# A two-layer expert block with attention: weight and table loads in another order, and slot scatters grouped elsewhere

## The chip, the cores and the metric

The kernel runs on one core of a Trainium2 chip. The metric is the device time of one execution in microseconds. TensorE (PE) multiplies matrices, PEld is its weight load, VectorE is DVE, ScalarE is ACT, GpSimd is POOL and SyncE is SP. SP issues plain transfers from its queue; POOL issues the indirect ones (gathers, scatters, scatter-adds).

## The reference

```python
x = L0_attn_x                                  # 8 x 1024 tokens x 256, float32
x = x + 0.5 * ffn(layernorm(x), router_w, w1, w2, bias)
x = x + attn(layernorm(x), w_qkv, w_gated, w_proj, gn_weight, gn_bias)
x = x + 0.5 * ffn(layernorm(x), router_w, w1, w2, bias)

def ffn(x, router_w, w1, w2, bias):            # 8 experts, top 2, capacity tokens / 8 = 1024 each
    scores = softmax(xf @ router_w)
    expert_weights, top_experts = top_k(scores, 2)
    for k in range(2):
        # the first 1024 tokens of each expert, in token order
        h = gelu(einsum('ech,ehf->ecf', xe, w1))      # 256 -> 1024
        ye = einsum('ecf,efh->ech', h, w2)            # 1024 -> 256
        out += scatter_add(ye) * expert_weights[:, k][:, None]
    return out + bias
```

The attention is a retention layer: 16 heads of 16, rotated queries and keys, a decaying causal mask without a softmax, a group norm over each head and all of time, a gate silu(x @ w_gated.T) and a projection.

## The kernel before

The kernel has three stages one after another on one core: the first expert layer, the attention, the second expert layer. The normalisation and routing of the first layer come before it; those of the second are part of the attention stage.

**The expert stages.** `ffn(r)` exists once for each engine, with r = 0 and r = 1. The work is 16 passes over an expert (8 experts for the first choice, then 8 for the second), 2 groups of 512 slots each: 32 groups. A loop `pair(p)` covers GE = 4 groups j, that is two experts, and runs 8 times. The products are made in split form (a high and a low part in fp32r).

- *SP* loads w1 and w2 of the coming expert pass into `stg1` and `stg2` (1 MB each, one buffer each), and the slot table of a coming group into `tab[:, j]` (32 KB). `next_w1(q, e)` waits until the eight slices of w1 of pass q-1 have been split (`f.w1l`), `next_w2(q, e)` the same for w2. The table of group j is loaded again for the next loop once `f.add` says that this group's scatter-add has landed. All of it is in one queue, in program order.
- *POOL*, in `pair`: `gather` reads the 512 rows of the group three ahead into `xe` (4 indirect transfers, line 428), when the table has landed and TensorE has read the old rows; `add` adds the group's results to the output rows (4 transfers, line 447), when they have been weighed and the adds before have landed. In the first three loops (`late`) `second_slot` weaves in the scatters of the second choice's slot entries (line 381), six per group until all 64 are out.
- *PE*, in `pair`: for each of 8 slices fj the down-products of group g (line 650, 12 matmuls) and the up-products of group g+1 (line 639, 6 matmuls); after slice 5 the transposes of the gathered rows of group g+2 (line 628). `up` of slice fj waits for the GELU of slice fj-2, whose PSUM bank it takes.
- *ACT*, in `pair`: per slice the GELU of group g+1 (line 1105), then in even groups the cast of a slice of w1 of the next pass (line 1109), in odd groups of w2 (line 1112). Before the first of each eight it waits for the raw weights, `f.w1raw` or `f.w2raw`. At the end of a group it weighs and evacuates the results (line 1122).
- *DVE* makes the low parts: of the weights (lines 1664, 1668), of the rows (1659) and of the hidden values (1672, 1676).

With r = 1 the last two batches' output rows are also stored by SP at the start of the stage (`output_store`, line 339); the last one waits for POOL's `half_bias(B - 1, j)`, which stands behind the second gather.

**The attention stage.** Each engine has a hand-written order `sequence(b)`, run for b = -1 to 7, and then `drain()`. A sequence works on batch b's eight tiles n and, between them, on the front of batch b+1, the output of batch b-1 and the routing of b-2. On POOL the order holds:

- `rotated(n)` (line 490), the last addition of the rotation of queries and keys; it waits for VectorE's products, and TensorE's `turn(n)` waits for it;
- the small powers of the norms (line 374), `half_bias` (line 393);
- `slots(b, j)` (line 381): two of the eight slot scatters of a batch's first choice. `slots(b, 0)` first waits for `R[1].pay`, which VectorE gives with the slot numbers `idx` (line 1598, in `slot_entries`). The scatters are wanted only by the second expert stage.

VectorE issues `slot_entries(1, b - 2)` right behind `rotate(n + 7)`.

Of the kernel before, what the change touches and what calls it, by code (L numbers as in the profile page):

```python
# [11 lines left out]
B, T, C = 8, 1024, 256  # L12
N = B * T
NT = T // P
# [4 lines left out]
E, TOPK, FF = 8, 2, 1024  # L19
# [5 lines left out]
NP = TOPK * E // 2  # L25
# [52 lines left out]
def macaron_kernel(nc, x_in, w_qkv, w_gated, w_proj, gn_w, gn_b, router_w, w1, w2, f_bias,  # L78
# [3 lines left out]
    with ctx:  # L82
# [113 lines left out]
        def held(eng, sem, value):  # L196

            eng.wait_ge(sem, value)
            eng.sem_inc(S0.passed, 1)
# [5 lines left out]
        def _(sp):  # L205
# [64 lines left out]
            def ffn(r):  # L270
                f = F[r]
                tab_t = slot_d[r].rearrange("(g p t) w -> g p t w", p=P, t=GT)

                def next_w1(q, e):
                    sp.wait_ge(f.w1l, q * FJ)
                    sp.dma_start(stg1[:], w1_t[e, :, :, :]).then_inc(f.w1raw, 16)

                def next_w2(q, e):
                    sp.wait_ge(f.w2l, q * FJ)
                    sp.dma_start(stg2[:], w2_t[e, :, :, :]).then_inc(f.w2raw, 16)  # L280

                def pair(p, wraps):

                    for j in range(GE):
                        q = p * 2 + j // 2 + 2
                        if j % 2 == 0:
                            next_w1(q, q - wraps)
                        else:
                            next_w2(q, q - wraps)

                        held(sp, f.add, p * (GE * GT * 16) + (j + 1) * GT * 16)
                        sp.dma_start(tab[:, j, :, :], tab_t[p * GE + GE + j, :, :, :]).then_inc(tabs[j], 16)

                tabs = [f.tab0, f.tab1, f.tab2, f.tab3]
                if r == 0:
                    sp.wait_ge(S0.acc_z, 16)
                    sp.wait_ge(S0.out_z, 16)
                    sp.wait_ge(S0.xn_z, 16)
                sp.wait_ge(R[r].scat, B * NT * 16)
                for j in range(GE):  # L300
                    sp.dma_start(tab[:, j, :, :], tab_t[j, :, :, :]).then_inc(tabs[j], 16)
                next_w1(1, 1)
                next_w2(1, 1)
                if r == 1:
                    output_store(B - 2)
                    output_store(B - 1)
                with sp.Fori(0, NP // 2 - 1) as p:
                    pair(p, 0)
                sp.wait_ge(R[r].scat1, B * NT * 16)
                pair(NP // 2 - 1, E)  # L310
                with sp.Fori(NP // 2, NP - 1) as p:
                    pair(p, E)

            ffn(0)

# [19 lines left out]
            def output_store(b):  # L336

                sp.wait_ge(R[1].half, (b + 1) * (NT // 2))
                sp.dma_start(out_w[b, :, :, :], rows_of(b)[:]).then_inc(R[1].stored, 16)
# [17 lines left out]
            ffn_weights(1)  # L357
            residual_store(B - 1)
            ffn(1)
            sp.wait_ge(F[1].add, NG * GT * 16)  # L360

# [4 lines left out]
        def _(pool):  # L366
# [9 lines left out]
            def scatter(r, b, some):  # L376

                if 0 in some:
                    held(pool, R[r].pay, b + 1)
                for n in some:  # L380
                    pool.indirect_dma_start(  # L381
                        out=slot_d[r], out_offset=bass.IndirectOffsetOnAxis(ap=idx[:, b, n:n + 1], axis=0),
                        in_=pay_rows[:, b, 2 * n:2 * n + ROW], in_offset=None, bounds_check=SLOTS - 1, oob_is_err=False)\
                        .then_inc(R[r].scat if n < NT else R[r].scat1, 16)

            def half_bias(b, j):

                if not 0 <= b < B:
                    return
                pool.wait_ge(R[1].xn, b * NT + 2 * j + 2)  # L390
                two = slice(2 * j, 2 * j + 2)
                x = rows_of(b)
                pool.tensor_tensor(x[:, two, :], x[:, two, :], hbias[:].unsqueeze(1).to_broadcast([P, 2, C]), ALU.add).then_inc(R[1].half, 1)
# [89 lines left out]
            def rotated(n):  # L483

                if not 0 <= n < B * NT:
                    return
                pool.wait_ge(A.qk_r, n + 1)
                if n >= 2:
                    pool.wait_ge(A.st, 2 * (n - 2) + 2)
                pool.tensor_tensor(qk[:, n % 2, :], rt1[:, n % 2, :], rt2[:, n % 2, :], ALU.add).then_inc(A.roped, 1)  # L490

            def first_output(b):

                if not 0 <= b < B:
                    return
                pool.wait_ge(A.y_r, b * NT + 1)
                if b >= 1:
                    pool.wait_ge(A.yg, b * KC)
                pool.tensor_copy(yT[:, :, 0:P], y0[:]).then_inc(A.moved, 1)

            def head_power(b):

                if not 0 <= b < B:
                    return
                pool.wait_ge(A.v_r, nth[1]["variances", b, 0])
                pool.tensor_tensor(gsm[:, 3, :], gsm[:, 2, :], K_["mhalf"][:, 0:KC], ALU.pow).then_inc(A.grs, 1)

            def front_power(b):
                if 0 <= b < B:
                    power(A, lnf, b)  # L510

            def residual_power(b):
                if 0 <= b < B:
                    power(R[1], lnr, b)

            def slots(b, j):

                if 0 <= b < B:
                    scatter(1, b, (2 * j, 2 * j + 1))

            def sequence(b):

                n = b * NT
                rotated(n + 2)
                head_power(b - 1)
                half_bias(b - 2, 2)
                rotated(n + 3)
                first_output(b)
                half_bias(b - 2, 3)
                rotated(n + 4)  # L530
                slots(b - 3, 1)
                rotated(n + 5)
                front_power(b + 1)
                slots(b - 3, 2)
                rotated(n + 6)
                slots(b - 3, 3)
                rotated(n + 7)
                rotated(n + 8)
                residual_power(b - 1)
                slots(b - 2, 0)  # L540
                rotated(n + 9)
                half_bias(b - 1, 0)
                half_bias(b - 1, 1)

            def drain():

                head_power(B - 1)
                for j in range(1, NT // 2):
                    slots(B - 3, j)
                residual_power(B - 1)  # L550
                for j in range(NT // 2):
                    slots(B - 2, j)
                for j in range(NT // 2):
                    slots(B - 1, j)
                half_bias(B - 2, 2)
                half_bias(B - 2, 3)

            pool.wait_ge(S0.slot1, 16)
            for b in range(-1, B):
                sequence(b)  # L560
            drain()
            ffn(1)

# [1565 lines left out]
```

## Time and profile before

| | |
|---|---|
| three runs | 2357.43, 2367.85 and 2370.43 us (median 2367.85) |
| the profiled execution | 2357.43 us, of which the span of the trace is 2355.6 |
| granted TensorE clock, mean | 0.975 |
| PE, PEld busy | 91%, 80% |
| DVE, ACT, POOL busy | 57%, 43%, 50% |
| first expert stage, attention, second expert stage | about 150 to 930, 930 to 1560, 1560 to 2356 us |

All times in the rows are microseconds from the span's start, unless marked ns. In a row of the timeline the number behind the start is how long the work took; "x8" joins eight instructions, and the bracket says how long the engine stood idle before it and who ended that. `L428` is line 428 of the kernel. In a row of stretches the numbers are the busy time of PE, PEld, DVE, ACT and POOL with the number of instructions, then the granted clock, the busy share of the 16 transfer engines and GB/s.

### The profile page before, as it was taken

To read this page: it belongs to the slowest core of one execution; us is meant where nothing else is said; L and a number is where in the kernel's file an instruction comes from. 1 tells how busy PE (TensorE), PEld (TensorE's weight loads), DVE (VectorE), ACT (ScalarE), POOL (GpSimd) and SP (SyncE) were. 2 spreads that over 40 slices of the span, in tenths; PEclk is the share of its full clock that TensorE was granted. 3 is DMA by queue.
4 is the path that set the end of the run, shared out by engine and by line. 5 is a ranking of instruction groups with operands and counts; after the bars stand their busy time and mean duration, and the time that the engine had idled before them with its cause. 6 is when DMAs were issued, how large, how long until landed. Compare 5 with 4: busy or idle time off the path is not lost.

```text
span 2355.6 us, 57424 instructions
## 1 busy us (share of the span) xinstructions
PE 2154.4 (91%) x22468; PEld 1894.0 (80%) x22468; DVE 1341.5 (57%) x3312; ACT 1008.1 (43%) x2149; POOL 1169.9 (50%) x911
## 2 busy tenths in 40 slices
PE   6749999999999996899999999729999999999997
PEld 5739998899999996677777777529998899999997
DVE  7745555455555552578778887635554455555552
ACT  4433443444444441446555555324343344444442
POOL 4754667654444443223344454364766764444443
PEclk9999999999999998999999999859999999999999
DMA  8532343444344433112111121132434354434342
GB/s 336 192 104 68 80 100 82 81 109 100 81 101 82 99 62 79 58 39 74 57 57 58 57 76 75 57 120 50 94 81 97 81 111 86 97 84 98 83 82 28
DMA packets 129223, 209.41 MB, mean 89 GB/s; under 512 B 24876, under 2 KB 105328, under 8 KB 122864
## 3 DMA queue, kind: packets, MB, share of 16 engines
q0 software_dynamic: 57344, 69.21, 17.6%
q1 hardware_dynamic: 71696, 137.62, 16.7%
q8 instruction: 132, 2.16, 0.4%
q14 instruction: 51, 0.42, 0.1%
HBM read 136.03 MB, written 72.88 MB: 89 GB/s over the span
## 4 chain that ended last, share of the span: by engine, by line
PE 40%; issue 6%; POOL 5%; DVE 4%; DMA 3%; ACT 1%; POOLq 0%; another core or an unknown queue 0%; SPq 0%; DVEq 0%; ACTq 0%
PE bank L639 10%; PE bank L650 10%; PE bank L723 10%; PE bank L811 3%; POOL out_rows L447 2%; POOL slot_table L381 2%; DMA out_rows<-yb,tab 2%; PE bank L844 2%; PE bank L779 1%; PE bank L794 1%; PE bank L829 1%; PE bank L628 1%; PE bank L883 1%; DMA tab<-slot_table 1%; POOL xe L428 1%
## 5 line engine op out<-in xcount | busy, mean ns | idle before, releaser
L1105 ACT ACTIVATE h<-bank 128x512 f32<-128x512 f32 x512 | 305.9, 597 | 873.5 <-PE bank L639 804.2
L1672 DVE CAST hh<-h 128x512 fp32r<-128x512 f32 x512 | 224.1, 438 | 715.3 <-ACT h L1105 628.1
L650 PE MATMUL bank<-w2h,hh 128*128 128x256 f32 x2048 | 582.5, 284 | 0.0
L650 PE MATMUL bank<-w2h,hl 128*128 128x256 f32 x2048 | 579.8, 283 | 0.0
L650 PE MATMUL bank<-w2l,hh 128*128 128x256 f32 x2048 | 579.7, 283 | 0.0
L428 POOL DMA_INDIRECT xe<-xn_rows,tab x256 | 274.8, 1073 | 344.5 <-issue 225.4
L639 PE MATMUL bank<-xh,w1h 128*128 128x512 f32 x1024 | 406.6, 397 | 4.2 <-DVE xl L1659 4.2
L650 PEld LDWEIGHTS bank<-w2h,hh 128*128 128x128 f32 x2048 | 391.5, 191 | 19.1
L639 PE MATMUL bank<-xl,w1h 128*128 128x512 f32 x1024 | 405.7, 396 | 0.0
L650 PEld LDWEIGHTS bank<-w2l,hh 128*128 128x128 f32 x2048 | 391.7, 191 | 17.1
L639 PE MATMUL bank<-xh,w1l 128*128 128x512 f32 x1024 | 399.8, 390 | 0.0
L650 PEld LDWEIGHTS bank<-w2h,hl 128*128 128x128 f32 x2048 | 391.5, 191 | 0.0
L1676 DVE TENSOR_TENSOR hl<-h,hh 128x512 fp32r<-128x512 f32 x512 | 350.4, 684 | 1.1
L381 POOL DMA_INDIRECT slot_table<-pay,idx x256 | 289.2, 1130 | 100.7 <-issue 75.1
L447 POOL DMA_INDIRECT out_rows<-yb,tab x128 | 211.3, 1651 | 171.2 <-issue 146.7
L447 POOL DMA_INDIRECT acc<-yb,tab x128 | 211.3, 1651 | 169.2 <-issue 109.3
L490 POOL TENSOR_TENSOR qk<-rt 128x512 f32<-128x512 f32 x64 | 88.4, 1381 | 287.0 <-DVE rt L1753 252.8
L639 PEld LDWEIGHTS bank<-xh,w1l 128*128 128x128 f32 x1024 | 193.2, 189 | 44.3
L639 PEld LDWEIGHTS bank<-xh,w1h 128*128 128x128 f32 x1024 | 195.2, 191 | 30.1 <-issue 4.9
L639 PEld LDWEIGHTS bank<-xl,w1h 128*128 128x128 f32 x1024 | 195.2, 191 | 21.5
L628 PE MATMUL bank<-cst,xe 128*128 128x128 f32 x512 | 69.2, 280 | 64.0 <-DMA xe<-xn_rows,tab 64.0
L628 PEld LDWEIGHTS bank<-cst,xe 128*128 128x128 f32 x512 | 60.9, 144 | 74.9 <-issue 54.8
(209 smaller groups left out, 3311.2 us busy)
## 6 DMA issues: line engine op xcount, KB each, us to landing
stg<-in_L_ffn_w SPq DMA_DIRECT2D x64, 1024.0 KB
xb<-acc SPq DMA_DIRECT2D x9, 1024.0 KB, 8.3
xa<-in_L_attn_x SPq DMA_DIRECT2D x8, 1024.0 KB, 14.1
xn_rows<-xa SPq DMA_DIRECT2D x8, 1024.0 KB
xn_rows<-xn_r SPq DMA_DIRECT2D x8, 1024.0 KB
xr<-acc SPq DMA_DIRECT2D x7, 1024.0 KB
out_rows<-xr SPq DMA_DIRECT2D x7, 1024.0 KB
slot_table<-pay,idx POOLq DMA_INDIRECT x256
```

Of the source, the lines that this page charges most:

```text
L381: pool.indirect_dma_start(out=slot_d[r], out_offset=bass.IndirectOffsetOnAxis(ap=idx[:, b, n:n + 1], axis=0), in_=pay_rows[:, b, 2 * n:2 * ...
L428: pool.indirect_dma_start(out=xe[j % 2][:, t, :], out_offset=None, in_=xn_d, in_offset=bass.IndirectOffsetOnAxis(ap=tabu[:, j, t, 0:1], ax ...
L447: pool.indirect_dma_start(out=dst, out_offset=bass.IndirectOffsetOnAxis(ap=tabu[:, j, t, 0:1], axis=0), in_=yb[j % 2][:, t, :], in_offset= ...
L490: pool.tensor_tensor(qk[:, n % 2, :], rt1[:, n % 2, :], rt2[:, n % 2, :], ALU.add).then_inc(A.roped, 1)
L628: last = pe.transpose(bank[6 + k][:, t * P:(t + 1) * P], xe[j % 2][:, t, k * P:(k + 1) * P], ident)
L639: last = pe.matmul(bank[fj % 2][:], a[:, k, w], c[j % 2][:, k, :], start=(n == 0), stop=(n == 5))
L650: last = pe.matmul(o, a[:, fj, s], c[:, fj, :], start=(fj == 0 and n == 0 and t % 2 == 0), stop=(fj == FJ - 1 and n == 2), skip_group_chec ...
L723: last = pe.matmul(out, a(k), c(k), start=(n == 0), stop=(n == 3 * KC - 1))
L811: last = pe.matmul(bank[3 + x][s, half * P:(half + 1) * P], qkT[rows, n % 2, KC + half, s], qm[rows, n % 2, half, :, s], start=True, stop= ...
L1105: act.activation(h32[fj % 2][:], bank[fj % 2][:], ACT.Gelu_apprx_tanh).then_inc(f.gelu, 1)
L1672: dve.tensor_copy(hh[:, fj, :], h32[fj % 2][:]).then_inc(f.hh, 1)
L1676: dve.tensor_tensor(hl[:, fj, :], h32[fj % 2][:], hh[:, fj, :].bitcast(fp32), ALU.subtract).then_inc(f.hl, 1)
```

## The change

It has two independent parts, both a new order of the same instructions.

*SP, in the expert stages.* Before, the weight loads run ahead of the loop by w1(1) and w2(1), and in the loop w1(2p+2), table 0, w2(2p+2), table 1, w1(2p+3), table 2, w2(2p+3), table 3 follow. After, only w1(1) is ahead of the loop, and the loop has w2(2p+1), table 0, w1(2p+2), table 1, w2(2p+2), table 2, w1(2p+3), table 3; w2(15) stands behind the last loop. With r = 1 the two output stores therefore come ahead of w2(1).

*POOL, in the attention stage.* In each sequence three pairs of scatters of batch b-3, which stood singly behind rotated(n+4), (n+5) and (n+6), are gone. Three pairs of batch b-2 stand together behind rotated(n+7), and the fourth where the first was. The drain has one batch's three pairs less.

```diff
                     for j in range(GE):
-                        q = p * 2 + j // 2 + 2
+                        q = p * 2 + j // 2
                         if j % 2 == 0:
-                            next_w1(q, q - wraps)
+                            next_w2(q + 1, q + 1 - wraps[j])
                         else:
-                            next_w2(q, q - wraps)
+                            next_w1(q + 2, q + 2 - wraps[j])
...
                 next_w1(1, 1)
-                next_w2(1, 1)
                 if r == 1:
                     output_store(B - 2)
                     output_store(B - 1)
                 with sp.Fori(0, NP // 2 - 1) as p:
-                    pair(p, 0)
+                    pair(p, (0, 0, 0, 0))
                 sp.wait_ge(R[r].scat1, B * NT * 16)
-                pair(NP // 2 - 1, E)
+                pair(NP // 2 - 1, (0, E, E, E))
                 with sp.Fori(NP // 2, NP - 1) as p:
-                    pair(p, E)
+                    pair(p, (E, E, E, E))
+                next_w2(TOPK * E - 1, E - 1)
...
                 rotated(n + 4)
-                slots(b - 3, 1)
                 rotated(n + 5)
                 front_power(b + 1)
-                slots(b - 3, 2)
                 rotated(n + 6)
-                slots(b - 3, 3)
                 rotated(n + 7)
+                slots(b - 2, 0)
+                slots(b - 2, 1)
+                slots(b - 2, 2)
                 rotated(n + 8)
                 residual_power(b - 1)
-                slots(b - 2, 0)
+                slots(b - 2, 3)
                 rotated(n + 9)
...
                 head_power(B - 1)
-                for j in range(1, NT // 2):
-                    slots(B - 3, j)
                 residual_power(B - 1)
```

## Rows read from the trace of the kernel before

**Rows 1.** Busy time in one stretch of the first expert stage.

```profile
200.00:300.00 100.00, 100.00 (x649) 90.97 (x648) 52.57 (x112) 42.21 (x96) 64.80 (x51) 1.00 0.40 87
```

**Rows 2.** Timeline of ACT: weighings that end groups, in both stages.

```profile
202.52 1.56 ACT L1122 ACTIVATE yb<-bank,tab 128x256 f32<-128x256 f32 x4
...
466.50 1.56 ACT L1122 ACTIVATE yb<-bank,tab 128x256 f32<-128x256 f32 x4
...
1621.91 1.56 ACT L1122 ACTIVATE yb<-bank,tab 128x256 f32<-128x256 f32 x4
...
1785.99 1.56 ACT L1122 ACTIVATE yb<-bank,tab 128x256 f32<-128x256 f32 x4
...
1886.53 1.56 ACT L1122 ACTIVATE yb<-bank,tab 128x256 f32<-128x256 f32 x4
```

**Rows 3.** Timeline of SP: issues of tables, weights and an output store.

```profile
471.71 0.34 SPq L292 DMA_DIRECT2D tab<-slot_table  x1
...
1567.85 0.58 SPq L339 DMA_DIRECT2D out_rows<-xr  x1
...
1638.85 0.36 SPq L292 DMA_DIRECT2D tab<-slot_table  x1
...
1715.89 0.33 SPq L292 DMA_DIRECT2D tab<-slot_table  x1
...
1867.39 0.33 SPq L292 DMA_DIRECT2D tab<-slot_table  x1
1868.04 0.38 SPq L276 DMA_DIRECT2D stg<-in_L_ffn_w  x1
1891.70 0.33 SPq L292 DMA_DIRECT2D tab<-slot_table  x1
...
1969.41 0.33 SPq L292 DMA_DIRECT2D tab<-slot_table  x1
```

**Rows 4.** Timeline of PE: first transposes of the two expert stages.

```profile
160.78 1.94 PE L628 MATMUL bank<-cst,xe 128*128 128x128 f32 x8 [21.61 <-DMA xe<-xn_rows,tab]
...
1579.63 1.94 PE L628 MATMUL bank<-cst,xe 128*128 128x128 f32 x8 [32.55 <-DMA xe<-xn_rows,tab]
```

**Rows 5.** Short stretches behind the weights issued at 1868.04.

```profile
1871.00:1872.00 1.00, 1.00 (x9) 0.93 (x8) 0.00 (x0) 0.55 (x2) 0.69 (x2) 1.00 1.00 414
...
1873.00:1873.50 0.50, 0.50 (x4) 0.41 (x3) 0.45 (x1) 0.00 (x0) 0.29 (x1) 1.00 0.00 0
```

**Rows 6.** Timeline of ACT: the start of group 2, second stage.

```profile
1647.37 0.60 ACT L1105 ACTIVATE h<-bank 128x512 f32<-128x512 f32 x1 [0.46 <-PE bank L639]
1647.87 0.41 ACT L1109 ACTIVATE w1h<-stg 128x256 fp32r<-128x256 f32 x1
1650.19 0.60 ACT L1105 ACTIVATE h<-bank 128x512 f32<-128x512 f32 x1 [1.92 <-PE bank L639]
```

**Rows 7.** Timeline of POOL: the first group's fourth gather, both stages.

```profile
155.96 1.01 POOL L428 DMA_INDIRECT xe<-xn_rows,tab  x1 [0.30 <-issue]
...
1571.76 1.01 POOL L428 DMA_INDIRECT xe<-xn_rows,tab  x1 [0.30 <-issue]
```

**Rows 8.** The chain that ended last: a fourth gather in group 10.

```profile
1875.98 2.82 DMA xe<-xn_rows,tab
```

**Rows 9.** Timeline of DVE and POOL in two batches of the attention stage.

```profile
1191.55 0.98 POOL L381 DMA_INDIRECT slot_table<-pay,idx  x1 [0.30 <-issue]
...
1197.87 0.17 DVE L1598 TENSOR_TENSOR idx<-sel 128x16 uint32<-128x16 f32 x1
...
1198.09 1.26 POOL L490 TENSOR_TENSOR qk<-rt 128x512 f32<-128x512 f32 x1 [1.22 <-PE bank L794]
1215.05 1.31 POOL L490 TENSOR_TENSOR qk<-rt 128x512 f32<-128x512 f32 x1 [15.70 <-DVE rt L1753]
...
1249.88 2.77 DVE L1856 TENSOR_TENSOR ygl<-yg,ygh 128x1024 fp32r<-128x1024 f32 x1
...
1253.17 2.06 DVE L1856 TENSOR_TENSOR ygl<-yg,ygh 128x1024 fp32r<-128x1024 f32 x1
```

## The prediction

> **What bounds the kernel now.** I read the page first, then the time in stretches of 100 us, then the dates of three engines inside the two expert stages, and last what TensorE waits for.
>
> The stretches say where to look. In the expert stages TensorE is busy for 100 of every 100 us [rows 1], except at their ends and in one stretch of each, which the next view sizes. So a moved transfer costs nothing there until somebody stands still for it, and the places to read are the few where TensorE does.
>
> ScalarE ends each group of 512 slots with the weighing at line 1122. In the second expert stage the first weighing starts at 1621.91 and the eighth at 1785.99: 164.08 / 7 = 23.44 us a group, TensorE's own pace. The twelfth should start at 1621.91 + 11 x 23.44 = 1879.75 and starts at 1886.53: 6.8 us are lost up to there. In the first stage the same sum is 202.52 + 11 x 23.44 = 460.36 against 466.50: 6.1 us lost [rows 2]. These 12.9 us are all that this stretch of the two stages has to give.
>
> They come from GpSimd's cycle. While the second choice's slot scatters are woven in (groups 0 to 10), a group takes GpSimd longer than 23.44 us. Sync issues the reload of a table the moment the scatter-add before it has landed, so the dates of the reloads are the cycle: from 1638.85 (group 0) to 1891.70 (group 10) it is 252.85 / 10 = 25.29 us [rows 3]. In this stretch GpSimd falls back 1.85 us per group against TensorE, and at the end the gathered rows come too late.
>
> The tables are not late because of the weights: at 1867.39 Sync issues the table, and at 1868.04 the weights behind it, which had been free to go [rows 3]. What holds the tables there is the adds.
>
> The other stop is at the start of a stage. TensorE stands still for 32.55 us before the first transposes of the second stage, and a gather ends that wait [rows 4].
>
> **The change, Sync's part.** Per loop it issues the same 4 weight loads and 4 table loads. Today the load that stands ahead of the table of group g is the one that ScalarE wants at the start of group g+3 (at the loop's entry g+2), so it has a group to spare. After the change the load wanted at the start of group g+2 is issued behind the table of group g. Nothing is queued behind a waiting weight load that suffers, since its own condition (the old weights split) is long true. The new thing is that weights wait for a scatter-add.
>
> When would they land? The weights issued at 1868.04 behind the table of 1867.39 show as 414 GB/s at 1871, and at 1873.0 the transfer engines are empty [rows 5]. From the table's issue to landed weights: 5.6 us.
>
> When are they wanted? The first cast of w1 for group 2 is at 1647.87 [rows 6], so for group 12 it is at 1647.87 + 10 x 23.44 = 1882.27 without a stall. That cast follows the weighing's date by 1647.87 - (1621.91 + 23.44) = 2.52; for the first stage it is due at 202.52 + 2.52 + 11 x 23.44 = 462.88.
>
> What covers a late arrival? ScalarE has made the group's first GELU before it waits. TensorE can still do the second and third up-products and the down-products up to the fourth: two steps of 1650.19 - 1647.37 = 2.82 us [rows 6], and about half a step, 1.4 us, for the last down-product, together 7.0. Of these 0.5 has passed when the cast normally starts; the cast (0.41) and a GELU (0.60) must still fit in. That leaves 5.5, and I allow 0.2 of it for hand-overs: 5.3 us.
>
> I expect a gain in the cycle itself. In the first three intervals weights run beside GpSimd's transfers, (1715.89 - 1638.85) / 3 = 25.68 us; in the seven after them they follow the table as they will after the change, (1891.70 - 1715.89) / 7 = 25.12 [rows 3]. I take 3 x 0.56 = 1.7 us off by group 10, once per stage. Bounds: nothing, and 3.
>
> Second stage, group 12: 1891.70 - 1.7 + 5.6 - 5.3 - 1882.27 = 8.0 us of lateness, in place of 6.8: +1.2. First stage: 471.71 - 1.7 + 5.6 - 5.3 - 462.88 = 7.4 in place of 6.1: +1.3. The two waits don't add: TensorE stops a little in each of groups 7 to 12 for the weights, and then the gathered rows are in time. Bounds per stage: no added lateness, and the cover absent (+5.3). I take the middle because the cover is read from a steady rhythm. Once the scatters are done, the weights are early: the table of 1969.41 (group 14) puts them at 1975.0, and group 16 wants them at 1882.27 + 6.78 + 4 x 23.44 = 1982.8.
>
> **The start of the second stage.** Sync now issues both output stores there before w2(1). Today w1, w2 and an output store (1 MB each) are issued within 1 us, the last at 1567.85 [rows 3]. The fourth gather of the first group, issued at 1571.76, lets TensorE begin at 1579.63: 7.87 us. In the first stage only w1 and w2 lie beside it, and the same step takes 160.78 - 155.96 = 4.82 us [rows 4, 7]. After the change w2(1) waits behind the last store, which waits for GpSimd's bias additions until some 11 us after the gather, so 2 MB lie beside the gathers here too. I take 7.87 - 4.82 = 3.0 us off, all on the path, since the chain runs through this landing. Bounds: nothing (if the store is the slow part), and 7.87 less the 2.82 of such a gather with little beside it [rows 8], 5.0. w2(1) is wanted over 40 us later, so its own delay costs nothing.
>
> The Trainium skill (DMA: Bandwidth & Descriptors, "Issuing engines are not separate DMA queues") says that transfers issued from different engines interleave on the same 16 transfer engines. This trace agrees: the same gather takes 4.82 us beside 2 MB of Sync's and 7.87 beside 3. With a path of its own for the gathers this term would be zero.
>
> **The change, GpSimd's part.** In each batch of the attention stage six slot scatters move: they were three pairs in the next batch, and now stand together behind the rope addition n+7. They need the batch's slot numbers, written at 1197.87, while that addition starts at 1198.09. The next rope addition starts at 1215.05 and waits for VectorE until then [rows 9]. A scatter is 0.98 us with 0.30 ahead of it [rows 9], so six are about 7.7 us, from 1199.4 to 1207.1, in a gap of 15.7. Cost: 0, hidden behind VectorE's and TensorE's own work. With that cover gone TensorE would wait up to 7.7 us in each of 6 batches. The pair left behind keeps its place, and at the stage's end GpSimd has six scatters less in a stretch where it then waits for VectorE's variance: 0.
>
> Where the scatters leave, they lay beside VectorE's subtraction at line 1856, which takes 2.77 us, while its twin takes 2.06 [rows 9]. I count nothing, because TensorE runs through that stretch.
>
> The Trainium skill (SBUF — State Buffer, "Who interferes with whom") says that a VectorE instruction with two SBUF inputs and a GpSimd instruction that reads SBUF exclude each other. The stretched row agrees in kind. What the rule would give is the third rival.
>
> **Sum.** +1.3 + 1.2 - 3.0 = -0.5 us on the profiled execution (span 2355.6, time 2357.43): 2356.9. That execution is the lowest of three runs; their median is 10.4 above it. Applied to the median: 2367.85 - 0.5 = 2367.3. I call up to 0.5% (11.8 us) no change, about what a measurement here can tell: the three runs lie 13 us apart.
>
> **The rivals.**
> 1. *The late weights stay hidden*, and the gathers still end last. Only the start's gain is left: -3.0, 2364.8. For it: the added lateness is just over 1 us a stage. Against it: it needs 1.3 us more cover. Chance 0.17.
> 2. *Slower: the late weights find no cover.* If TensorE stops as soon as ScalarE waits, each stage loses 5.3 us more: -0.5 + 10.6 = +10.1, 2378.0; with the cycle's gain absent too, 3.4 more, 2381.4. It decides from the first group whose weights land behind the due cast, group 5 or 6. For it: ScalarE's wait holds up every later GELU. Against it: the order of TensorE's instructions. Chance 0.19, three quarters of it beyond 0.5%.
> 3. *The scatters' collision was on the path.* 2.77 - 2.06 = 0.7 us in each of 5 batches, -3.5: 2363.8. Against it: TensorE's busy share there. Chance 0.10.
> 4. *Faster: GpSimd's cycle falls to TensorE's pace* once weights no longer run beside its adds. Then the 12.9 us of both stages vanish, and the start's 3.0: 2352. It needs 1.85 us off every group. Against it: in the last seven intervals the weights already lie there, and the cycle is 25.12. Chance 0.10.
>
> My forecast has 0.44. With rivals 1 and 3 and a quarter of rival 2 this makes 0.76 for within 0.5%; 0.14 slower, 0.10 faster.
>
> **Range.** Downwards: rival 1 with the start at its bound and rival 3 on top, -8.5, gives 2359.4; I go to the lowest run shown, 2357. Upwards rival 2, to 2381. Rival 4 and the end of rival 2 are left out, under 2 in 10. The likeliest case alone spans 2363 to 2371.
>
> **What would show it.** Right: in groups 7 to 12 ScalarE's first cast waits for a transfer of weights, and TensorE stops just before the fourth up-product; its waits for gathered rows before group 12 are gone; the twelfth weighing is 7 to 9 us late; the fourth gather is followed by TensorE after about 5 us; the rope additions n+7 and n+8 stay some 17 us apart. Wrong: a twelfth weighing over 12 us late (no cover) or under 5 (the cycle changed), or a later rope addition n+8.

## The result, and the profile after

| | before | after |
|---|---|---|
| median | 2369.14 us (4 runs) | 2401.78 us (4 runs) |
| ratio | | 1.0145, interval 1.0122 to 1.0167 |
| the profiled execution, its span | 2357.43, 2355.6 | 2399.01, 2397.2 |

The changed kernel is slower by 32.6 us in the medians, where I had forecast -0.5. It is outside the range. By dates in the two traces the 41.6 us between the two spans lie as follows. Up to the first load of the attention stage (932.78 before, 937.01 after): +4.2. From there to the last slot numbers of VectorE (1549.75, 1589.13): +35.2. From there to the first weighing of the second expert stage: -1.4. The rest of that stage: +3.6.

The expert stages first. These rows answer to [rows 2, 3]: weighings of ScalarE, tables and weights of Sync, of the changed kernel.

```profile
203.17 1.56 ACT L1120 ACTIVATE yb<-bank,tab 128x256 f32<-128x256 f32 x4
...
470.12 1.56 ACT L1120 ACTIVATE yb<-bank,tab 128x256 f32<-128x256 f32 x4
...
1659.90 1.56 ACT L1120 ACTIVATE yb<-bank,tab 128x256 f32<-128x256 f32 x4
...
1927.92 1.56 ACT L1120 ACTIVATE yb<-bank,tab 128x256 f32<-128x256 f32 x4
```

```profile
219.54 0.36 SPq L292 DMA_DIRECT2D tab<-slot_table  x1
...
348.47 0.34 SPq L292 DMA_DIRECT2D tab<-slot_table  x1
348.90 0.38 SPq L280 DMA_DIRECT2D stg<-in_L_ffn_w  x1
...
472.60 0.34 SPq L292 DMA_DIRECT2D tab<-slot_table  x1
```

The twelfth weighing is 470.12 - 203.17 - 11 x 23.44 = 9.1 us late in the first stage and 10.2 in the second, where [rows 2] had 6.1 and 6.8. The cycle of the tables is (472.60 - 219.54) / 10 = 25.31 in the first stage and 25.35 in the second, no shorter than before (25.27 and the 25.29 of [rows 3]).

What the view of waits says of ScalarE in the changed kernel (engine, tile, line, who ended the wait: us in total, times, longest):

```profile
ACT w2h L1110 <- DMA stg<-in_L_ffn_w: 53.9, 10, 8.4
...
ACT w1h L1107 <- DMA stg<-in_L_ffn_w: 42.8, 10, 6.7
...
ACT vz L1195 <- remote: 38.7, 6, 7.1
```

The first two rows are the forecast's late weights. The third is new, and it comes six times, once for each batch whose scatters moved. "remote" is the profile's word for a releaser that it can't name. GpSimd in one of these batches, the answer to [rows 9]:

```profile
1211.33 1.29 POOL L490 TENSOR_TENSOR qk<-rt 128x512 f32<-128x512 f32 x1 [3.59 <-PE bank L792]
1213.54 1.05 POOL L381 DMA_INDIRECT slot_table<-pay,idx  x1 [0.92 <-DVE idx L1596]
...
1220.01 0.97 POOL L381 DMA_INDIRECT slot_table<-pay,idx  x1 [0.30 <-issue]
```

Six scatters stand from 1213.54 to 1220.98, as forecast in number, length and place. The next rope addition starts at 1234.79, 23.5 us behind the one of 1211.33, where [rows 9] had 1215.05 - 1198.09 = 17.0. The distances in the five batches that have both are 24.5, 23.5, 23.4, 22.1 and 23.9. GpSimd is not the late one: the scatters end 13.8 us before that addition, and GpSimd then waits for VectorE. The other three engines, in the same batch:

```profile
1215.54 0.48 ACT L1207 ACTIVATE qm<-bank,cst 128x256 f32<-128x256 f32 x1
...
1216.29 0.21 DVE L1771 TENSOR_TENSOR state<-bank,cst 128x64 f32<-128x64 f32 x1
1216.32 0.45 PE L809 MATMUL bank<-qm,qkT 32*64 32x128 f32 x3 [0.31 <-issue]
...
1217.08 0.41 PE L809 MATMUL bank<-qm,qkT 32*64 32x128 f32 x2 [0.30 <-issue]
...
1218.25 0.28 PE L721 MATMUL bank<-wTh,xnl 128*128 128x256 f32 x1
...
1219.22 0.39 PE L721 MATMUL bank<-xnh,wTl 128*128 128x512 f32 x1 [0.45 <-issue]
...
1222.23 0.69 DVE L1761 TENSOR_TENSOR aw<-bank,cst 128x512 f32<-128x512 f32 x1 [5.73 <-remote]
1222.31 0.38 ACT L1195 ACTIVATE vz<-bank 128x256 f32<-128x256 f32 x1 [6.29 <-remote]
...
1222.84 0.36 PE L721 MATMUL bank<-wTh,ygh 128*128 128x256 f32 x1 [2.29 <-ACT vz L1195]
```

VectorE's product at line 1761 and ScalarE's copy at line 1195 wait for counts of TensorE alone. TensorE has made what they want by 1217.5 and 1218.5, but both start within 0.1 us of each other at 1222.2, some 4 us late and 1.2 us after the last scatter has ended. TensorE meanwhile goes in pieces, with gaps that nothing explains. The chain that ended last runs through it:

```profile
1215.65 0.36 ACT qm L1207
1216.02 6.27 another core or an unknown queue
...
1222.31 0.39 ACT vz L1195
```

The hold isn't the whole of the 6.5 us by which this distance grew. TensorE had stood idle or gone in pieces from 1216 on, and then its granted clock fell (the number behind the brackets of POOL):

```profile
1223.00:1224.00 1.00, 1.00 (x9) 1.00 (x9) 0.97 (x4) 1.00 (x3) 0.00 (x0) 0.99 0.00 0
1224.00:1225.00 1.00, 1.00 (x23) 0.78 (x29) 0.12 (x1) 0.16 (x1) 0.00 (x0) 0.50 0.00 0
...
1227.00:1228.00 1.00, 1.00 (x21) 0.86 (x21) 0.33 (x1) 0.62 (x2) 0.00 (x0) 0.81 0.00 0
```

That is 3.4 us at half clock with TensorE fully busy, which costs 1.7 us. The clock fell to half in all five batches (for 3.4 us in three of them, for some 10 us in the first and the last); before, it stayed at 1.00 between the two additions of [rows 9].

The start of the second expert stage answers to [rows 4, 7]:

```profile
1611.19 1.01 POOL L428 DMA_INDIRECT xe<-xn_rows,tab  x1 [0.30 <-issue]
```

```profile
1616.71 1.51 PE L626 MATMUL bank<-cst,xe 128*128 128x128 f32 x6 [30.24 <-DMA xe<-xn_rows,tab]
```

From the fourth gather to TensorE it is 5.5 us now, 7.9 before.

### The profile page after: what moved, and what is told of

Read it like the earlier page. It is cut to its first block, busy times and chain, and to the rows that moved or that the text cites. A ratio compares the mean times of both kernels' runs of the same rounds, so it can differ in the third digit from the quotient of the medians.

```text
span 2397.2 us, 57448 instructions
## 1 busy us (share of the span) xinstructions
PE 2179.2 (91%) x22468; PEld 1910.7 (80%) x22468; DVE 1343.5 (56%) x3312; ACT 1008.4 (42%) x2149; POOL 1151.6 (48%) x911
## 4 chain that ended last, share of the span: by engine, by line
PE 39%; issue 6%; POOL 5%; DVE 4%; DMA 3%; another core or an unknown queue 2%; ACT 1%; POOLq 0%; SPq 0%; DVEq 0%; ACTq 0%
PE bank L637 10%; PE bank L648 10%; PE bank L721 9%; PE bank L809 3%; POOL out_rows L447 2%; POOL slot_table L381 2%; DMA out_rows<-yb,tab 2%; PE bank L842 2%; PE bank L777 1%; PE bank L792 1%; PE bank L881 1%; PE bank L626 1%; PE bank L827 1%; DMA tab<-slot_table 1%
## 5 line engine op out<-in xcount | busy, mean ns | idle before, releaser
L381 POOL DMA_INDIRECT slot_table<-pay,idx x256 | 271.0, 1059 | 105.0 <-issue 75.4
L1666 DVE TENSOR_TENSOR w2l<-stg,w2h 128x256 fp32r<-128x256 f32 x256 | 106.0, 418 | 53.7 <-issue 30.7
L1662 DVE TENSOR_TENSOR w1l<-stg,w1h 128x256 fp32r<-128x256 f32 x256 | 106.0, 419 | 42.7 <-ACT w1h L1107 31.5
```

The lines of the kernel that those rows point to most:

```text
L381: pool.indirect_dma_start(out=slot_d[r], out_offset=bass.IndirectOffsetOnAxis(ap=idx[:, b, n:n + 1], axis=0), in_=pay_rows[:, b, 2 * n:2 * ...
L1662: dve.tensor_tensor(w1l[:, :, w], stg1[:, :, w], w1h[:, :, w].bitcast(fp32), ALU.subtract).then_inc(f.w1l, 1)
L1666: dve.tensor_tensor(w2l[:, fj, :], stg2[:, fj, :], w2h[:, fj, :].bitcast(fp32), ALU.subtract).then_inc(f.w2l, 1)
```

## The experiments

Kernels that ran together, on one chip and beside the kernel before, are called a set here. It matters, because the sets turned out to be of two kinds. The differences within a set count, not those between sets.

### The two parts alone, the scatters spread, and a busy GpSimd (set 1)

e1 has only Sync's part of the diff, e2 only GpSimd's.

> Only the new order of Sync's loads; the attention stage as before. The profile of the changed kernel puts the loss of the expert stages at +3.5 and +3.5 us, 0.7 ahead of them, and the start of the second stage at -2.4: +5 us on the kernel before if the two parts of the change are independent. If instead the late weights only hurt together with the shifted attention stage, 0 or below.

> Only the new places of GpSimd's slot scatters; Sync's order as before. If the six scatters behind rotated(n+7) cost 5.9 us in each of six batches: +35 us, and the waits of ScalarE at vz and VectorE at aw that end on no named engine are there six times each. If the attention stage lost its time to Sync's part: 0.

e3 has the scatters early but pair by pair:

```diff
                 half_bias(b - 2, 2)
+                slots(b - 3, 2)
                 rotated(n + 3)
                 first_output(b)
                 half_bias(b - 2, 3)
+                slots(b - 3, 3)
                 rotated(n + 4)
-                slots(b - 3, 1)
                 rotated(n + 5)
                 front_power(b + 1)
-                slots(b - 3, 2)
                 rotated(n + 6)
-                slots(b - 3, 3)
                 rotated(n + 7)
+                slots(b - 2, 0)
                 rotated(n + 8)
                 residual_power(b - 1)
-                slots(b - 2, 0)
+                slots(b - 2, 1)
```

The pairs of the last batches in the drain follow suit.

> The scatters of batch b-2 start as early as in the changed kernel, behind rotated(n+7), but one pair stands behind each of n+7, n+8, and the two additions that open the next sequence. Theory A, what costs is that six scatters follow each other without a gap: within 4 us of the kernel before. Theory B, what costs is the place, scatters between rotated(n+7) and rotated(n+8): a third of the loss, about +12 us.

e4 leaves the scatters and adds work to GpSimd:

```diff
                 rotated(n + 7)
+                busy(b - 2, 7)
                 rotated(n + 8)
```

`busy(b, 7)` waits for the batch's slot numbers and then issues seven memsets of 128 x 1024.

> The scatters stand where they stood in the kernel before. Behind rotated(n+7) seven memsets of 128x1024 (0.95 us each, about 7 us of GpSimd work that moves nothing by transfer) are added. Theory A (the scatters themselves hold up the other engines): 0 to +3 us. Theory C (GpSimd is busy and something waits for it): about the same +30 to +35 us as six scatters.

| | median us | ratio to the kernel before (2358.25) |
|---|---|---|
| e1 Sync's part | 2361.46 | 1.0012 (1.0000 to 1.0023) |
| e2 GpSimd's part | 2359.98 | 1.0007 (0.9995 to 1.0019) |
| e3 spread | 2369.42 | 1.0055 (1.0036 to 1.0074) |
| e4 memsets | 2358.12 | 1.0003 (0.9990 to 1.0016) |

My first theory (each part keeps its own loss) fell: e2 has the same six scatters and costs nothing. In its trace the rope addition n+7 is at 1205.86 and n+8 at 1222.83, 17.0 us. The kernel before was faster here too, 2358 in place of 2369. With nothing lost in e2, e4 could not tell anything yet. e3's loss is another matter, and an ordinary one: one pair stands directly ahead of the rope addition n+3, ahead of which e2's GpSimd is idle for 1.1 us only. In the traces, about 1175 us, n+3 follows n+2 after 7.0 us in e3 and after 5.6 in e2.

### The changed kernel again, with a shift, and the output stores alone (set 2)

> The changed kernel once more, beside the kernel before on the same chip. Neither part alone cost more than 2.8 us. Theory D, the two parts together cost what neither does: +33 us again, with the same six stops of 6 us behind the six scatters. Theory E, the first comparison was special to its chip or its loading: the sum of the parts, +4 to +8 us.

e6 is the changed kernel with eight fulfilled waits more on Sync ahead of the attention stage.

> The changed kernel with eight more instructions on Sync just ahead of the attention stage (waits that are already fulfilled), which only shift Sync's later code and its place in time by under 1 us. Theory D1, the loss comes from how instruction or semaphore traffic happens to fall against the scatters: a loss clearly other than 33 us, perhaps none. Theory D2, it comes from the order of transfers alone: +33 us again.

```diff
                 next_w1(1, 1)
-                next_w2(1, 1)
                 if r == 1:
                     output_store(B - 2)
                     output_store(B - 1)
+                next_w2(1, 1)
```

> The kernel before, with only the two output stores at the start of the second expert stage moved ahead of w2(1). Loops and scatters as before. The fourth gather should be followed by TensorE after 5.5 us in place of 7.9: -2.4 us. If the gain belonged to the later w2 of the loop, 0.

e8 is e7 with GpSimd's part of the change.

> The same with the scatters where the changed kernel has them. By the sum of the parts +1.7 - 2.4 = about -1 us. If the six scatters stop the engines in any program whose Sync code differs from the one that was measured with them alone: +30 us.

| | median us | ratio to the kernel before (2369.18) |
|---|---|---|
| e5 the changed kernel | 2404.00 | 1.0150 (1.0127 to 1.0173) |
| e6 with the shift | 2405.88 | 1.0159 (1.0142 to 1.0176) |
| e7 stores first | 2368.41 | 0.9996 (0.9985 to 1.0008) |
| e8 the same, six scatters | 2396.49 | 1.0120 (1.0103 to 1.0137) |

The loss is back, and the shift does nothing to it. e8 against e7 is 28 us for the scatters, e5 against e8 is 7.5 us for the loops' order. e7's start takes 1585.29 to 1590.82, 5.5 us, but its median can't be told from the kernel before: 2.2 us are less than such a comparison resolves. e8 and e2 differ in one moved line of Sync's, and e8 loses 27.3 us where e2 lost 1.7. Either that line matters, or the set does.

### GpSimd's part again, with fewer scatters in a row (sets 3 and 4)

> GpSimd's part alone for the second time. In the first call it lost 1.7 us, on a chip where no engine's wait ended on an unnamed releaser; in the second call the same six scatters, with the two output stores moved as well, lost 27 us. Theory F, the chip decides (or where the program lies on it), not the program: where the kernel before takes about 2369 us, +28 to +30 us here too, with six stops; where it takes about 2358, +2. Theory D, this part needs another part of the change to hurt: within 5 us on any chip.

> The scatters of the batch start as early as in the changed kernel, but one pair behind each of four rope additions. Where f1 shows six stops: theory A, a run of six without a gap is what costs: no stop, and the 7 to 11 us that the first call showed for this order, in place of the 28 of f1. Theory B, the scatters in this place cost, each for itself: a third of f1's stops stay behind n+7.

> Scatters as before, and seven memsets of GpSimd behind n+7. Where f1 shows six stops: theory A, only scatters hold up the others: 0 to +3 us. Theory C, a busy GpSimd holds them up: near f1.

f4 has `slots(b - 3, 3)` behind n+6, `slots(b - 2, 0)` and `slots(b - 2, 1)` behind n+7 and `slots(b - 2, 2)` behind n+8.

> Two pairs behind n+7 in place of three; the third pair behind n+6 of the next sequence, the fourth behind n+8. Where f1 shows six stops of 6 us: if the stop grows with the run of scatters past a start, 2 to 4 us per batch, +12 to +24 us. If it is proportional to their number, 4 us per batch, +19 to +24. If it takes more than four in a row, 0 to +3.

> The changed kernel again. If this set is of the kind in which the kernel before takes about 2369 us: +33 us with six stops. If it is of the kind with about 2357: no stops, and only Sync's part is left, +3 to +6 us. A loss of 30 us in a set of the second kind would speak for an effect of the two parts together.

> Two pairs of scatters behind n+7. Where the kernel before takes about 2369 us: +12 to +24 us if the stops grow with the number of scatters, 0 to +3 if it takes more than four in a row. Else 0.

> Seven memsets behind n+7, scatters as before. Where the kernel before takes about 2369 us: 0 to +3 us if only scatters hold up the other engines, about +28 if a busy GpSimd does. Else 0.

| | median us | ratio to the kernel before |
|---|---|---|
| set 3 (before 2356.35): f1 GpSimd's part | 2356.79 | 0.9999 (0.9987 to 1.0011) |
| f2 spread | 2366.11 | 1.0036 (1.0023 to 1.0049) |
| f3 memsets | 2354.74 | 0.9990 (0.9976 to 1.0004) |
| f4 four scatters | 2356.28 | 1.0005 (0.9989 to 1.0021) |
| set 4 (before 2357.13): g1 the changed kernel | 2358.71 | 1.0006 (0.9993 to 1.0019) |
| g2 four scatters | 2358.01 | 1.0001 (0.9989 to 1.0013) |
| g3 memsets | 2359.01 | 1.0003 (0.9990 to 1.0017) |

g1 settles what e2 and e8 left open: the very kernel that lost 33 and 35 us loses 1.6 us here, which can't be told from nothing. It is not the program but the set. Set 3 ran on the same chip as set 2, so it isn't the chip either. ScalarE in g1, in the batch whose addition n+7 is at 1208.12:

```profile
1213.57 0.38 ACT L1195 ACTIVATE vz<-bank 128x256 f32<-128x256 f32 x1 [0.76 <-PE bank L721]
```

The same copy is released by TensorE after 0.76 us, with the same scatters beside it (1210.33 to 1217.77). I call a set *held* when traces in it have waits that end on "remote", and *free* when none has. Held: the first comparison and set 2. Free: sets 1, 3 and 4. But sets 3 and 4 couldn't answer what in a held set does the holding, since nothing was held in them.

### One kernel with another arrangement in each batch (sets 5 and 6)

Here one execution in a held set compares all arrangements. Behind rotated(n+7):

```diff
                 rotated(n + 7)
+                behind7(b - 2)
                 rotated(n + 8)
...
+            def behind7(b):
...
+                if b == 2:
+                    held(pool, R[1].pay, b + 1)
+                    fill(7)
+                elif b == 3:
+                    for j in range(3):
+                        for n in (2 * j, 2 * j + 1):
+                            scatter(1, b, (n,))
+                            fill(1)
+                    del todo[b][:3]
+                elif 0 <= b < B - 2:
+                    for _ in range({0: 3, 1: 2, 4: 1, 5: 3}[b]):
+                        left(b)
```

`fill(k)` issues k memsets of 128 x 1024, each awaited, and `left(b)` the next pair of the batch's scatters. The scatters left over are issued in pairs behind n+8 and n+4 to n+6.

> Behind rotated(n+7) stand, batch after batch: six scatters; four; seven memsets and no scatter; six scatters with a memset of 0.95 us after each; two scatters. The distance from n+7 to n+8 tells what each costs (17.0 us is the undisturbed one, 22.1 to 24.5 the one behind six scatters in the changed kernel's trace). In a set of the kind in which the kernel before takes about 2369 us: theory A, a run without gaps holds up the others once it is longer than some length: 23.5, 17 to 20, 17, 17 and 17 us. Theory A2, each scatter costs 1 us: 23.5, 21, 17, 23, 19. Theory C, a busy GpSimd holds them up: 23.5, 21, 23, 28, 19. In a set of the other kind: 17 in all five.

> The same kernel and the same numbers as for the first run of it: in a set in which the kernel before takes about 2369 us, the distances from n+7 to n+8 behind six scatters, four, seven memsets, six scatters with memsets between and two scatters are 23.5, 17 to 20, 17, 17, 17 us by theory A (a long run without gaps), 23.5, 21, 17, 23, 19 by theory A2 (each scatter costs), 23.5, 21, 23, 28, 19 by theory C (a busy GpSimd). Otherwise 17 in all five.

Set 5 was free (before 2358.18, h1 2354.55, ratio 0.9989, 0.9974 to 1.0005), set 6 held (before 2371.54, h2 2386.47, ratio 1.0072, 1.0037 to 1.0107, with three executions of each that count). The distances from n+7 to n+8, from the timeline of GpSimd:

| behind n+7 | h1 (free) | h2 (held) | held costs |
|---|---|---|---|
| 6 scatters in a row | 16.97 | 22.20 | 5.2 |
| 4 in a row | 16.98 | 21.41 | 4.4 |
| 7 memsets | 17.03 | 17.02 | 0 |
| 6 with memsets between | 17.92 | 17.94 | 0 |
| 2 in a row | 16.97 | 18.17 | 1.2 |

The rows of h2 for four scatters in a row, for seven memsets and for the six set apart, of which the first stands here:

```profile
1209.55 1.29 POOL L491 TENSOR_TENSOR qk<-rt 128x512 f32<-128x512 f32 x1 [3.59 <-PE bank L824]
1211.76 1.05 POOL L382 DMA_INDIRECT slot_table<-pay,idx  x1 [0.92 <-DVE idx L1628]
...
1215.68 0.97 POOL L382 DMA_INDIRECT slot_table<-pay,idx  x1 [0.30 <-issue]
1230.96 1.30 POOL L491 TENSOR_TENSOR qk<-rt 128x512 f32<-128x512 f32 x1 [14.31 <-DVE rt L1783]
...
1286.86 1.29 POOL L491 TENSOR_TENSOR qk<-rt 128x512 f32<-128x512 f32 x1 [3.59 <-PE bank L824]
1288.34 7.02 POOL L529 MEMSET idle<- 128x1024 f32 x7 [0.19 <-DVE idx L1628]
1303.88 1.28 POOL L491 TENSOR_TENSOR qk<-rt 128x512 f32<-128x512 f32 x1 [8.53 <-DVE rt L1783]
...
1357.41 1.31 POOL L491 TENSOR_TENSOR qk<-rt 128x512 f32<-128x512 f32 x1 [1.38 <-PE bank L824]
1359.62 0.99 POOL L382 DMA_INDIRECT slot_table<-pay,idx  x1 [0.91 <-DVE idx L1628]
1360.61 0.98 POOL L529 MEMSET idle<- 128x1024 f32 x1
1362.38 0.98 POOL L382 DMA_INDIRECT slot_table<-pay,idx  x1 [0.79 <-POOL idle L529]
...
1375.35 1.28 POOL L491 TENSOR_TENSOR qk<-rt 128x512 f32<-128x512 f32 x1
```

Each arrangement stands in one batch only. That the batch isn't what differs is seen in e7, also held: without scatters behind n+7 its distance is 17.0 us. Seven memsets in a row hold up nobody (theory C falls). In a row, a scatter costs 0.6 to 1.1 us by this table. With a memset between, and so 1.8 us from the end of one to the start of the next, six cost nothing beyond the free set's 17.9, in which GpSimd itself is 1 us late. So neither theory A (a threshold) nor A2 (each scatter costs, apart ones too) stands as I put it: two in a row cost less than four, but scatters that are set apart cost nothing. Whether it is the memset or the time between them that helps was not tested, nor any gap between 0.3 and 1.8 us. Six and four can't be ranked by one batch each, since six cost 5.1 to 7.5 us in the changed kernel. And the clock has a share here too: behind the four it stands at half for 3.4 us with TensorE busy, 1.7 of the 4.4 us, while behind the two it stays at 1.00.

```profile
1217.81 0.39 ACT L1227 ACTIVATE vz<-bank 128x256 f32<-128x256 f32 x1 [3.58 <-PE bank L753]
```

This is ScalarE behind the four. The scatters end at 1216.65, ScalarE goes on at 1217.8, again 1.2 us later. (Over all rows of four and six in the held traces the two engines go on 1.1 to 1.5 us after the last scatter.) Here the profile names TensorE as the releaser, so a hold need not show as "remote": the length of the wait is the sign.

### Every scatter by itself (set 7)

The version that this points to has one scatter between any two other GpSimd operations of a sequence, and e7's stores:

```diff
+                slot(b - 3, 2)
                 rotated(n + 4)
-                slots(b - 3, 1)
+                slot(b - 3, 3)
                 rotated(n + 5)
+                slot(b - 3, 4)
                 front_power(b + 1)
-                slots(b - 3, 2)
+                slot(b - 3, 5)
                 rotated(n + 6)
-                slots(b - 3, 3)
+                slot(b - 3, 6)
                 rotated(n + 7)
+                slot(b - 3, 7)
                 rotated(n + 8)
+                slot(b - 2, 0)
                 residual_power(b - 1)
-                slots(b - 2, 0)
+                slot(b - 2, 1)
```

> The kernel before with every scatter of the attention stage's loop by itself between two other GpSimd operations, and with the two output stores at the start of the second expert stage ahead of w2(1). The start's 2.2 us come off in any set. In a set in which the kernel before takes about 2369 us its four pairs per batch cost up to 1.2 us each by the pair behind n+7 of the mixed kernel; its attention stage measured 5 to 10 us longer than in the other sets, so -7 to -12 us in all. In a set in which it takes about 2357: -2 us. If GpSimd's order gets in the way of the rope additions, as with the spread pairs, 0 to +10.

2356.64 against 2355.17, ratio 1.0003 (0.9994 to 1.0013), in a free set. It gains nothing there, not even the 2 us of the start that I expected in any set (at its best bound the interval allows 1.4). Whether it gains in a held set was not measured.

## Why the prediction was wrong, point by point

**The step that failed** is "Cost: 0, hidden behind VectorE's and TensorE's own work". The number of scatters, their length (7.4 us for 7.7) and their place in GpSimd's gap were right. What was wrong is the assumption that work on an engine which nobody waits for costs nobody anything. I wrote that "with that cover gone TensorE would wait up to 7.7 us in each of 6 batches", and the size comes near: 5.1 to 7.5 us in each of the five batches that can be measured, +35.2 us over the attention stage. That nearness is luck. The gap in GpSimd's order was never gone, and the measured distances contain the time at half clock (1.7 us in the batch shown). In a held set the row of scatters stops engines that don't wait for it, TensorE too. In a free set the step holds: g1's distances are 17.0 to 17.4 us.

**The rivals** had no such case. The slower one (late weights without cover, 2378.0 to 2381.4) is not it. The third, a collision of scatters with VectorE, looked in the right direction with the wrong sign: I asked what the scatters leave, not what they do where they arrive. Its reading was wrong too. What stretches the subtraction at line 1856 is the rope addition n+4 (1248.57 to 1250.77), not the scatters behind it: in the kernel before one at 1108.74 takes 2.77 us with this addition beside it and no scatter, and with the scatters gone, in the changed kernel, the row still takes 2.77 to 2.80 us and its twin 2.05 to 2.11. So the row that I said agreed in kind speaks of the addition.

**Could the trace of before have told it?** In part. It has this row in its view of waits:

```profile
ACT h L1105 <- remote: 20.0, 6, 4.2
```

All six lie between 233 and 362 us, where GpSimd weaves scatters, gathers and adds, mostly with 0.3 us between them. One of them:

```profile
228.35 1.01 POOL L381 DMA_INDIRECT slot_table<-pay,idx  x1 [0.30 <-issue]
...
231.74 1.01 POOL L381 DMA_INDIRECT slot_table<-pay,idx  x1 [0.30 <-issue]
...
233.12 0.60 ACT L1105 ACTIVATE h<-bank 128x512 f32<-128x512 f32 x1 [4.24 <-remote]
```

With one core at work there is no other to wait for, so the row should have been asked for its cause. I read past it because TensorE didn't stop there. A second row lies in the attention stage itself:

```profile
DVE state L1773 <- remote: 5.7, 4, 1.5
```

```profile
1220.48 0.97 POOL L381 DMA_INDIRECT slot_table<-pay,idx  x1 [0.30 <-issue]
1221.13 0.22 DVE L1773 TENSOR_TENSOR state<-bank,cst 128x64 f32<-128x64 f32 x1 [1.38 <-remote]
```

VectorE waits there for TensorE's count, in four batches, and goes on while the second scatter of the pair behind n+8 still runs or within 0.5 us of its end. From n+8 to n+9 it is 8.28, 8.33, 8.13 and 8.11 us in these batches. In the free e1, which has the same attention stage, it is 7.22, 8.35, 7.22 and 7.21: in three of four batches two scatters in a row already cost 1 us before the change. What the trace could not tell is the second half, that the same program is free of it in other sets: there the change costs 1.6 us, inside the range.

**The expert stages.** Forecast: lateness 7.4 and 8.0 us where 6.1 and 6.8 had been, +1.3 and +1.2. Worked out in the same way from ScalarE's timeline in the profiled executions of all runs, the twelfth weighing is late by 8.6 and 8.2 us on average with the old order (15 executions, 5.9 to 10.4) and by 9.9 and 9.6 with the new one (5 executions, 9.0 to 10.7): +1.4 and +1.5. The difference is right within this spread, the levels are not, because I took them from one execution that lies near the good end of it. Between the two profiled kernels the same difference is therefore 3.0 and 3.4. Of its parts, the gain in the cycle (1.7 us in ten groups) isn't there between these two. Over the same executions the cycle is 25.41 and 25.37 us on average with the old order and 25.28 and 25.29 with the new one, 1.3 and 0.8 us in ten groups. The landing took 354.75 - 348.47 = 6.3 us in place of 5.6:

```profile
354.75 0.42 ACT L1110 ACTIVATE w2h<-stg 128x256 fp32r<-128x256 f32 x1 [7.40 <-DMA stg<-in_L_ffn_w]
```

TensorE has no work from 353.7 to 355.7, and behind this stop the granted clock fell:

```profile
355.00:356.00 1.00, 0.30 (x1) 0.30 (x2) 0.81 (x2) 0.95 (x3) 0.91 (x1) 1.00 0.04 8
...
357.00:358.00 1.00, 1.00 (x6) 0.90 (x4) 1.00 (x3) 0.62 (x2) 0.69 (x2) 0.50 0.26 94
358.00:359.00 1.00, 1.00 (x6) 1.00 (x6) 1.00 (x3) 0.50 (x2) 0.77 (x1) 0.50 0.47 131
359.00:360.00 1.00, 1.00 (x7) 1.00 (x6) 1.00 (x3) 0.00 (x0) 0.93 (x1) 0.50 0.07 8
360.00:361.00 1.00, 1.00 (x5) 0.81 (x5) 0.13 (x1) 0.00 (x0) 0.70 (x2) 0.80 0.00 0
```

TensorE is busy for 0.3 of the first of these microseconds. From 357 on three stand at 0.50, which is 1.2 GHz, and one at 0.80: 3.4 us at half speed, which cost 1.7 us of work. The weighings of 344.65 and 371.88 lie 27.2 us apart for 23.44. I had priced the stop and not what the clock takes after it.

**The start of the second stage.** Forecast 7.87 to 4.82 us, measured 5.5 in the profile after and 5.5 to 5.7 in e1, e5, e6, e7, e8, g1 and h3, against 7.6 to 8.1 in all with the old order: -2.2 for -3.0. That it is so in e7 shows that the later w2(1) alone does it.

**Of the signs I named**, the waits for weights, the vanished waits for gathered rows and the shorter start came true, and so did "a later rope addition n+8" on the list of what would be wrong. The twelfth weighings, 9.1 and 10.2 us late, lie just beyond the 7 to 9 that I gave for right.

## What to carry to other kernels

Price a run of indirect transfers on GpSimd by what it does to the other engines, not only by who waits for it: where these holds occur, two together cost up to 1.2 us, six 5 to 7, and six with a memset between any two nothing. Part of such a price is the lower clock behind the stop. A kernel whose scatters all stand apart (h3) was not measured there. A wait in a single-core trace whose releaser has no name is worth an explanation before anything is moved. And a gain or loss is measured best in several sets, beside the unchanged kernel each time: here the same two kernels differ by 1.5% or by nothing.
